# Tile 1 ahead of layer 2, the second group ahead of h2, GpSimd paced from tile 2 on

## The reference, cut to what matters

```python
x0 = emb[ids].reshape(2048, 1664)          # ids: 2048 x 26
x = x0
for i in range(3):
    x = x0 * (x @ cross_w[i])[:, None] + cross_b[i] + x
h = relu(x0 @ w1 + b1)                     # 1664 -> 1024
h = relu(h @ w2 + b2)                      # 1024 -> 512
h = relu(h @ w3 + b3)                      # 512 -> 256
y = sigmoid(concatenate([x, h], axis=1) @ out_w + out_b)
```

## Time and profile before

| | |
|---|---|
| median of 3 runs | 537.11 us (536.67 to 539.26) |
| time of the profiled execution | 536.77 us |
| its span, first to last instruction | 535.0 us |
| PE, PEld busy | 469.5 us (88%), 435.6 us (81%) |
| POOL busy | 379.1 us (71%), 407 instructions |
| DVE, ACT busy | 184.6 us (35%), 104.9 us (20%) |
| chain that ended last | PE 51%, ACT's queue 12%, POOL 10%, issue 9%, ACT 6%, DMA 6%, DVE 5% |
| mean granted clock of TensorE | 0.997 |

### The profile page before, as it was taken

How to read it: one execution, slowest core, us unless ns; L and a number is a source line. 1 busy time by engine, 2 the same in 40 slices (tenths; PEclk the granted TensorE clock), 3 DMA queues, 4 the chain that set the end, 5 groups by cost and what they waited for, 6 DMA issues and landing times.

```text
span 535.0 us, 11277 instructions
## 1 busy us (share of the span) xinstructions
PE 469.5 (88%) x2876; PEld 435.6 (81%) x2876; DVE 184.6 (35%) x383; ACT 104.9 (20%) x194; POOL 379.1 (71%) x407
## 2 busy tenths in 40 slices
PE   0088599999898999899898999989899898999997
PEld 0088389898888989798897989889798887989996
DVE  5464523314142322424232241423233142323325
ACT  6495501101011110111111020111011011101111
POOL 5777667577777777777777777777777777777720
PEclk9999999999999999999999999999999999999999
DMA  7992111011111111111111111111111111111100
GB/s 230 229 365 80 25 23 29 23 30 26 30 30 27 30 30 28 28 30 31 26 31 28 29 29 29 29 28 29 30 28 28 31 26 31 28 28 29 28 10 2
DMA packets 21730, 25.17 MB, mean 47 GB/s; under 512 B 11335, under 2 KB 12322, under 8 KB 21666
## 3 DMA queue, kind: packets, MB, share of 16 engines
q0 software_dynamic: 12800, 13.13, 11.9%
q1 hardware_dynamic: 6800, 11.01, 6.0%
q10 hardware_dynamic: 2066, 0.31, 0.3%
HBM read 24.41 MB, written 0.01 MB: 46 GB/s over the span
## 4 chain that ended last, share of the span: by engine, by line
PE 51%; ACTq 12%; POOL 10%; issue 9%; ACT 6%; DMA 6%; DVE 5%; POOLq 0%; DVEq 0%
PE l_bank L714 39%; ACTq L389 11%; POOL x_raw L341 10%; DMA x_raw<-in_L_rec_emb,idx 5%; PE x_bank L714 4%; PE x_bank L730 3%; PE h_bank L758 3%; ACT xT_hi L402 2%; ACT w_hi L359 2%; DVE x_raw L520 2%; ACTq L386 1%; DVE xT_lo L527 1%; PE l_bank L789 1%; ACT h_bank L369 1%; DVE h2T_lo L532 1%
## 5 line engine op out<-in xcount | busy, mean ns | idle before, releaser
L341 POOL DMA_INDIRECT x_raw<-in_L_rec_emb,idx x400 | 378.3, 946 | 132.1 <-issue 104.4
L714 PE MATMUL l_bank<-w_hi,xT_hi 128*128 128x342 f32 (+1 forms) x624 | 145.2, 333 | 8.0 <-DVE xT_lo L527 7.9
L714 PE MATMUL l_bank<-w_lo,xT_hi 128*128 128x342 f32 (+1 forms) x624 | 137.9, 321 | 0.0
L714 PE MATMUL l_bank<-w_hi,xT_lo 128*128 128x342 f32 (+1 forms) x624 | 137.9, 321 | 0.0
L714 PEld LDWEIGHTS l_bank<-w_hi,xT_hi 128*128 128x128 f32 x624 | 103.4, 190 | 12.8 <-DVE xT_lo L527 11.4
L714 PEld LDWEIGHTS l_bank<-w_lo,xT_hi 128*128 128x128 f32 x624 | 106.8, 190 | 0.0
L714 PEld LDWEIGHTS l_bank<-w_hi,xT_lo 128*128 128x128 f32 x624 | 106.5, 190 | 0.0
L527 DVE TENSOR_TENSOR xT_lo<-x_bank,xT_hi 128x512 fp32r<-128x512 f32 (+1 forms) x66 | 38.2, 578 | 164.5 <-ACT xT_hi L402 164.5
L402 ACT ACTIVATE xT_hi<-x_bank 128x512 fp32r<-128x512 f32 (+1 forms) x66 | 33.5, 507 | 262.7 <-PE x_bank L730 199.7
L730 PE MATMUL x_bank<-identity,x_raw 128*128 128x128 f32 x208 | 34.9, 280 | 44.1 <-DVE x_raw L520 27.1
L730 PEld LDWEIGHTS x_bank<-identity,x_raw 128*128 128x128 f32 x208 | 25.2, 142 | 53.1 <-issue 50.5
(11 more groups left out here) (90 smaller groups left out, 289.4 us busy)
## 6 DMA issues: line engine op xcount, KB each, us to landing
ids<-in_L_rec_emb SPq DMA_DIRECT2D x1152, 0.2 KB
ids<-in_L_rec_emb ACTq DMA_DIRECT2D x896, 0.2 KB
w_raw<-in_L_rec_w SPq DMA_DIRECT2D x18, 512.0 KB, 21.3
x_raw<-in_L_rec_emb,idx POOLq DMA_INDIRECT x400, 2.8
b_rows<-in_L_rec_b SPq DMA_DIRECT2D x1, 512.0 KB, 9.4
b_rows<-in_L_rec_b SPq DMA_DIRECT2D x1, 256.0 KB, 7.5
ids<-in_r_ids SPq DMA_DIRECT2D x1, 208.0 KB, 2.7
b_rows<-in_L_rec_b SPq DMA_DIRECT2D x1, 128.0 KB, 8.0
```

The lines of the kernel that those rows point to most:

```text
L341: pool.indirect_dma_start(out=dst, out_offset=None, in_=emb, in_offset=rows).then_inc(landed, 16)
L714: done = pe.matmul(bank[:, 0:b - a], x[:, k, :], w[:, k, a:b], start=(k == 0 and n == 0), stop=(k == last_k and n == 2))
```

## The change

- **SP and DVE, start.** The indices are loaded by two DMAs: the columns of the first eight fields (`FIRST`) first, with a semaphore of their own, then the rest. DVE waits for each by itself.
- **TensorE, tiles 0 and 1.** The transposes of x(1,0) go in front of the first half of layer 2 of tile 0; all four chunks of layer 1 of x(1,0), with the transposes of x(1,1) between them, go in front of its second half. From tile 2 on TensorE's order is as before.
- **ACT, DVE, end of tile 0.** Fills, copies and splits of x(1,0) and x(1,1) go between the late splits of weights.
- **ACT, DVE, every later tile.** The copy of x(t,1) goes in front of that of h2 of the tile before; the fill and the split of x(t,1) go in front of the split of h2.
- **ACT's fetches.** The 64 a tile are shared out as 12, 16, 8, 16, 12 instead of 8, 12, 4, 16, 12, 12. In tile 1 the first two shares stand together in front of the copy of h2.
- **GpSimd.** In tile 1 the waits on `chunk_done` are gone. From tile 2 on they are as before, and the wait for h2's transposes at field 2 now holds for tile 2 as well.

The diff:

```diff
-    ACT_SHARES = [8, 12, 4, 16, 12, 12]
+    ACT_SHARES = [12, 16, 8, 16, 12]
...
-    SLACK = {1: 2}
+    FIRST_PACED = 2
...
-            sync.dma_start(ids[:, :], r_ids.rearrange("(p t) f -> p (t f)", p=P)).then_inc(ids_loaded, 16)
+            by_row = r_ids.rearrange("(p t) f -> p (t f)", p=P)
+            sync.dma_start(ids[:, 0:FIRST], by_row[:, 0:FIRST]).then_inc(first_ids_loaded, 16)
+            sync.dma_start(ids[:, FIRST:TILES * F], by_row[:, FIRST:TILES * F]).then_inc(ids_loaded, 16)
...
-                if f == 2 and t > 2:
+                if f == 2:
                     pool.wait_ge(h2_transposed, t - 1)
...
-                        if t > 0 and f % FPK == 0 and f // FPK not in NOT_PACED:
-                            pool.wait_ge(chunk_done, max(1, PACED * t - BEHIND[f // FPK] - SLACK.get(t, 0)))
-                        if t > 1:
+                        if t >= FIRST_PACED and f % FPK == 0 and f // FPK not in NOT_PACED:
+                            pool.wait_ge(chunk_done, PACED * t - BEHIND[f // FPK])
+                        if t >= FIRST_PACED:
                             other_engines_turn(t, f)
...
                 h1_hi(0)
-                for n in LATE:
+                x_hi(1, 0)
+                for n in LATE[:-1]:
                     split_hi(n)
+                x_hi(1, 1)
+                split_hi(LATE[-1])
 
             def step(t):
                 fetch(ACT_SHARES[0])
                 x_hi(t, 0)
                 fetch(ACT_SHARES[1])
-                h2_hi(t - 1)
-                fetch(ACT_SHARES[2])
                 x_hi(t, 1)
-                fetch(ACT_SHARES[3])
-                x_hi(t, 2)
...
+                rest_of_step(t)
 
             def last_step(t):
                 x_hi(t, 0)
+                x_hi(t, 1)
                 h2_hi(t - 1)
-                x_hi(t, 1)
                 x_hi(t, 2)
...
+            def rest_of_step(t):
+                h2_hi(t - 1)
+                if t > 1:
+                    fetch(ACT_SHARES[2])
+                x_hi(t, 2)
+                if t == 1:
+                    fetch(ACT_SHARES[2])
+                if t in SP_TILES:
+                    sp_place(t)
+                if t in ACT_TILES:
+                    act_place(t)
+                fetch(ACT_SHARES[3])
+                x_hi(t, 3)
+                fetch(ACT_SHARES[4])
+                h1_hi(t)
+
             first_step()
             act.wait_ge(sp_idx_ready, 1)
-            for t in range(1, TILES - 1):
+            fetch(ACT_SHARES[0])
+            fetch(ACT_SHARES[1])
+            rest_of_step(1)
+            for t in range(2, TILES - 1):
                 step(t)
...
+                make_whole(1, 0)
                 dve.wait_ge(consts_summed, 1)
...
                 h1_lo(0)
-                for n in LATE:
+                x_lo(1, 0)
+                make_whole(1, 1)
+                for n in LATE[:-1]:
                     split_lo(n)
+                x_lo(1, 1)
+                split_lo(LATE[-1])
 
             def begin(t):
                 make_whole(t, 0)
                 x_lo(t, 0)
                 l2_out(t - 1)
-                h2_lo(t - 1)
                 make_whole(t, 1)
                 x_lo(t, 1)
+                h2_lo(t - 1)
...
                 transpose_h1(0)
+                transpose_x(1, 0)
+                l2(0, range(0, HB))
+
+            def begin_second():
+
+                l1(1, 0, slice(0, 2))
+                transpose_x(1, 1)
+                l1(1, 0, slice(2, None))
+                l2(0, range(HB, K2))
+                l1(1, 1, slice(0, 1))
+                transpose_h2(0)
+                transpose_x(1, 2)
+                l1(1, 1, slice(1, None))
+                rest_of_step(1, 2)
...
             first_step()
-            for t in range(1, TILES - 1):
+            begin_second()
+            for t in range(2, TILES - 1):
                 step(t)
             last_step(TILES - 1)
```

More of the change, by code:

```diff
@@ L217, in splits_done @@
             return 2 * (n + 1)
+        first_ids_loaded = sem("first_ids_loaded")
         ids_loaded = sem("ids_loaded")
@@ L640, in begin @@
                 l2_out(t - 1)
-                h2_lo(t - 1)
                 make_whole(t, 1)
                 x_lo(t, 1)
+                h2_lo(t - 1)
             def step(t):
[L646 to L649, removed]
+                if t > 1:
+                    begin(t)
+                    make_whole(t, 2)
+                else:
+                    l2_out(0)
+                    make_whole(1, 2)
+                    h2_lo(0)
+                x_lo(t, 2)
+                make_whole(t, 3)
+                x_lo(t, 3)
                 l1_out(t)
@@ L684, in to_indices @@
                 dve.sem_inc(idx_ready, 1)
+            dve.wait_ge(first_ids_loaded, 16)
+            to_indices(0, FIRST)
             dve.wait_ge(ids_loaded, 16)
-            to_indices(0, FIRST)
             to_indices(FIRST, TILES * F)
@@ L849, in begin, with rest_of_step @@
                 l1(t, 0, slice(-ahead(t), None))
-            def step(t):
-                begin(t)
-                for g in range(1, NG):
+            def rest_of_step(t, first_g):
+                for g in range(first_g, NG):
                     l1(t, g, slice(0, -ahead(t)))
@@ L859, in step @@
                 l3(t - 1)
+            def step(t):
+                begin(t)
+                rest_of_step(t, 1)
             def last_step(t):
```

## The result

The change takes 543.4 us (median of four runs, 541.23 to 545.45) beside 537.8 us of the kernel before on the same chip: ratio 1.0099, interval [1.0053, 1.0144]. In six more runs it took 543.74 us, ratio 1.0104 [1.0074, 1.0134]. It is slower by 1%; the forecast was 537.8 us, its range ended at 539.9. Ratios here are against runs of the kernel before on the same chip; the batches of experiments ran on different chips, so kernels of different batches are compared by ratio. The profiled execution is one of the shorter ones: 541.44 us, span 539.6.

What follows compares the result with a forecast made beforehand. The prediction took POOL's release in tile 2, a fixed run of gathers and PE's tail as the bound: 535.0 + 0.8 - 0.5 + 0.7 = 536.0, with 1.8 outside the span 537.8 us; range 533.4 to 539.9.

Steps and rivals of the forecast that it cites:

- The bound: Whole span: POOL's release at 97.24 in tile 2, a fixed run of gathers at 1.25 us each, PE's tail from 480.70.
- The prediction's own sign of being wrong: POOL passing field 16 of tile 2 before 95, or its gathers waiting again in later tiles.
- Tile 1: PE stalls 5.1 us before x(1,2), then 4 (2.3 if the clock lowers) before x(1,3); x(2,0) transposed 0.8 us later.
- the second rival's first part: Tile 1: PE at 1.2 GHz from 88.2 after the second stall, POOL released 1.7 us later; 539.5 us, chance 0.13.
- The first rival: Tile 1: ACT lets the copies through, POOL runs unheld from 89.4; 529 us, half way 533.8; chance 0.20.
- The start: First index DMA shrinks from 208 to 4 KB: gain between 0 and 1.3 us, 0.5 taken for the whole chain.
- Tiles 2 to 13: The 1.1 us a tile before x(t,1) go, the wait before x(t,2) grows by as much; booked at nothing.
- The clock rival: Clock falls in tile 1's second stall: 539.5 us; longer middle-tile waits cost again only in the last tile; chance 0.13.
- The tail: Tiles 14 and 15: 0.1 us lost at h1's copy, 0.6 before layer 3 of tile 14; 0.7 in the sum.

Runs made afterwards that it cites:

- the second profile: Profile from six further runs of the unaltered change, timed beside runs with one part undone; 543.74 us, ratio 1.0104.
- the old steady order's run: The change, but from tile 2 on ACT and DVE handle h2 ahead of x(t,1) with the former fetch shares; 539.64 us, ratio 1.0015.
- the change again: The change, nothing altered, six more runs against the kernel before; 543.74 us, ratio 1.0104.
- the steady order alone: The kernel before with only x(t,1)'s fill, copy and split ahead of h2's and shares 12, 16, 8, 16, 12; 539.35 us, ratio 1.0016; repeated, 1.0032.

## Why the prediction was wrong, by its own steps

- **The bound.** Right that POOL's release, the run of gathers and PE's tail set the end, and the balance above closes by these terms but for 0.9 us. Wrong that the run is fixed: 1.25 us each holds only while PE keeps ahead of POOL's waits. The prediction's own sign of being wrong came, gathers that "wait again in later tiles".
- **Tile 1.** Right in its places. The copy of h2 was worked out for 76.4 and came at 75.19, that of x(1,2) at 75.69 for 76.9: 28 fetches took 10.87 us, not the 12.1 worked out from shares that each stood between copies. The stall before x(1,2) is 4.72 us for 5.1. The second is 1.02 us (2.00 in the second profile) where 2.3 was said for a lowered clock. The clock did fall, and the release, forecast at +0.3 with the earlier start, came at -0.3 in one profile and +1.4 in the other. Where a second slow stretch follows the second stall (the old steady order's run, the change again) it is the later one, as the second rival's first part has it.
- **The first rival's price** was right: with the fetches out of the way POOL runs unheld, at 89.5 for the 89.4 worked out, and the time is 530.06 for 529. That the numbers meet so closely is partly luck: the first gather came 0.9 us earlier than in the sum, POOL had one gather more, and tile 14's fetches were gone as well. Its chance was rightly small for this change. The Trainium skill, DMA: Bandwidth & Descriptors, section "Issuing engines are not separate DMA queues", calls the sequencer's time to initiate a DMA usually small relative to the DMA. The runs disagree for DMAs of 0.2 KB: 64 fewer on ACT's queue in each of tiles 1 and 14 are worth, in the change, 1.0104 - 0.9904 of 538 us, about 11 us, though POOL gathers one field more. Most of that is tile 1's: the release came at 89.98 for 98.63 in the second profile of the change.
- **The start**: the first gather came 0.8 us earlier, the first transposes at 24.98 for 26.02, 1.0 us (0.6 in the second profile of the change); 0.5 was taken, 1.3 was the bound.
- **Tiles 2 to 13: the step that failed.** "The wait for POOL before x(t,2) grows by as much. Booked at nothing, POOL being the cover." The wait did grow, and the 1.1 us did go. What the step left out is that two short waits of 1.1 and up to 1.6 us (1.31 in the earlier trace rows), which had left the clock alone in that execution, become one of 2 to 4 us, in which it fell in five tiles; PE's slack against POOL's field 16 is then spent, and POOL is held. This term, booked at nothing, measured +3.2 us, and +3.6 in the second profile (417.43 for 413.86).
- **The clock rival** had the mechanism and the wrong place and size. It gave 539.5 us for tile 1 and said that longer waits in middle tiles "would cost as much again only in the last". In the middle they cost the most. The Trainium skill, TensorE: Matmul & The Clock Gate, section "HAM oscillation — how this bites in real kernels", describes a clock that falls at every wait of a loop; the prediction set against it that the trace showed this once. The trace of the change shows it in every other tile: the rule was nearer. The profile before could not speak against it, as its longest wait in tiles 2 to 14 was 1.6 us.
- **The tail**: +0.8 us for +0.7, with 0.39 us idle before layer 3 of tile 14 for 0.6.

The later landing of the gather before x(14,2), +0.9 us in the balance, is not explained: the median landing was 3.1 us in this profile, 2.8 before, and 2.7 to 3.1 in the other kernels. In the second profile of the change PE does not wait before x(14,2) at all. Whether the change makes gathers land later is not shown.

## What to carry to other kernels

Where idle time moves, ask for the length of the piece that it joins: short waits that do no harm can make one that lowers the clock, and its cost then lands on whoever waits for TensorE next. Before a wait is "covered" by another engine, look up where that engine waits in turn, and how much slack it has there. And when a change clears one engine's order, see first whether the next queue lets the gain through: here taking ACT's fetches out of tiles 1 and 14 was worth more than the whole reordering. A profile is one execution: look at the clock of the other runs too before calling a wait harmless.

## What was not expected of the hardware

A slow stretch of the clock in tiles 1 to 14 lasted about 3.4 or 6.8 us in all these profiles. A wait of 1.9 us in tile 0, which all thirteen profiles have, was followed by a slow stretch in five of them, and the same wait before x(3,2), 3.58 and 4.02 us, was followed by full speed in one kernel and by half in another. Adding matmuls whose results nobody reads made the kernel faster (1.0041 of the kernel before, for 1.0104). Runs of one program differ by up to 7.7 us (536.93 to 544.62 for the steady order alone, at clocks of 0.980 and 0.959): most of it goes with the granted clock.
